# K and Q projections of a cross-attention kernel: the last 64 features with the weights' high and low parts in one stationary

## The reference, cut to what matters

```python
q = _split_heads(hidden_states @ w_q, HEADS)            # (16*256, 320) @ (320, 320)
k = _split_heads(text @ w_k, HEADS)                     # (.., 512) @ (512, 320)
v = _split_heads(text @ w_v, HEADS)
out_text = _merge_heads(_sdpa(q, k, v))
out_ip = _merge_heads(_sdpa(q, k_ip, v_ip, mask=mask_ip))
out = (out_text + out_ip) @ w_out + b_out + residual
```

## Time and profile before

| | |
|---|---|
| three timed runs | 524.48, 525.25, 527.94 us, median 525.25 |
| the profiled execution | 523.65 us, span 521.8 us (1.85 us lie around the span) |
| mean granted TensorE clock | 0.984 |
| TensorE matmul busy | 476.5 us, 91% |
| VectorE busy | 380.1 us, 73% |
| ScalarE busy | 275.9 us, 53% |
| GpSimd busy | 134.6 us, 26% |
| stages, from the span's start | lone tiles to 57 us, batch -1 to 79, batches 0 to 11 to 429, the rest to 521.8 |

### The profile page before, as it was taken

The page is one execution under the profiler, slowest core; times in us unless marked ns, Lnnn a source line. Parts: engine busy times, 40 slices in busy tenths (PEclk is TensorE's granted clock), DMA queues, the critical chain, the costliest instruction groups (busy, mean ns, idle before and its releaser), DMA issues.

```text
span 521.8 us, 11039 instructions
## 1 busy us (share of the span) xinstructions
PE 476.5 (91%) x4306; PEld 321.1 (62%) x4306; DVE 380.1 (73%) x687; ACT 275.9 (53%) x355; POOL 134.6 (26%) x208
## 2 busy tenths in 40 slices
PE   2998668999999999999999999999999998798895
PEld 2786535676667756676667756676667755454542
DVE  4833466877877797877877797877877779899732
ACT  3643025555655565455655555455655456466670
POOL 6250000313221140313222140314212220432431
PEclk9999797999999999999999999999999999999998
DMA  8999985858593967758593958757594937273011
GB/s 270 333 227 314 360 289 180 286 174 265 166 335 102 328 194 202 263 167 276 179 333 93 334 186 221 245 169 268 179 302 129 319 125 244 87 262 109 9 53 50
DMA packets 94036, 112.61 MB, mean 216 GB/s; under 512 B 14320, under 2 KB 72736, under 8 KB 93984
## 3 DMA queue, kind: packets, MB, share of 16 engines
q1 hardware_dynamic: 92960, 109.57, 65.9%
q0 software_dynamic: 1024, 2.34, 1.9%
HBM read 73.28 MB, written 38.63 MB: 214 GB/s over the span
## 4 chain that ended last, share of the span: by engine, by line
issue 56%; POOL 21%; PE 10%; DMA 5%; SPq 3%; DVE 2%; ACT 1%; POOLq 0%; ACTq 0%
POOL o_turned L411 10%; POOL o_all L416 7%; POOL x_all L405 4%; PE score_q L650 1%; DMA v_rows<-v_out 1%; PE pv L762 1%; PE score_q L651 1%; PE score_q L652 1%; DMA max_rows<-row_buf 1%; SPq L226 1%; PE pj L771 1%; DMA probs<-in_wk 1%; PE score_t L748 1%; DMA raw<-in_ctxT 1%; DMA q_parts<-qk_out 1%
## 5 line engine op out<-in xcount | busy, mean ns | idle before, releaser
L562 DVE TENSOR_REDUCE max_cols<-score_q 128x4 fp32r<-128x992 f32 x155 | 183.1, 1181 | 86.1 <-PE score_q L693 85.1
L494 ACT ACTIVATE probs<-score_t 128x1024 f32<-128x1024 f32 x160 | 163.3, 1021 | 145.8 <-PE score_t L748 145.8
L762 PE MATMUL pv<-probs,v_cur 128*32 128x256 f32 x1920 | 120.2, 383 | 0.6 <-ACT probs L494 0.6
L411 POOL TENSOR_TENSOR o_turned<-o_turned,inv_cols 128x256 f32<-128x256 f32 x80 | 53.9, 674 | 155.3 <-DVE inv_cols L606 155.3
L771 PE MATMUL pj<-wo_sb,o_all 128*128 128x320 f32 x192 | 70.5, 477 | 9.6 <-DVE out_sb L618 5.8
L762 PEld LDWEIGHTS pv<-probs,v_cur 128*32 128x32 f32 x1920 | 54.3, 109 | 39.1 <-issue 1.0
L405 POOL TENSOR_TENSOR x_all<-x_all,bias_sb 128x640 f32<-128x640 f32 x16 | 24.9, 1559 | 202.0 <-DMA x_all<-in_x 202.0
L748 PE MATMUL score_t<-q_stack,k_stack 64*128 64x256 f32 x440 | 55.8, 332 | 11.2 <-ACT probs L494 7.9
L748 PEld LDWEIGHTS score_t<-q_stack,k_stack 64*128 64x128 f32 x440 | 33.1, 186 | 52.2 <-issue 36.1
L603 DVE STREAM_TRANSPOSE o_turned<-o_all 128x512 f32<-128x512 f32 x80 | 55.8, 698 | 11.9 <-ACT o_all L486 11.9
L486 ACT ACTIVATE o_all<-pv 128x512 f32<-128x512 f32 x80 | 47.8, 598 | 27.3 <-PE pv L762 27.3
(11 more groups left out here) (152 smaller groups left out, 635.2 us busy)
## 6 DMA issues: line engine op xcount, KB each, us to landing
k_stack<-k_parts SPq DMA_DIRECT2D x33, 320.0 KB, 5.2
q_stack<-q_parts SPq DMA_DIRECT2D x33, 320.0 KB, 6.6
v_rows<-v_out SPq DMA_DIRECT2D x32, 320.0 KB, 6.7
v_cur<-v_rows SPq DMA_DIRECT2D x16, 640.0 KB
q_parts<-qk_out SPq DMA_DIRECT2D x32, 256.0 KB, 4.0
k_parts<-qk_out SPq DMA_DIRECT2D x32, 248.0 KB, 5.9
raw<-in_ctxT SPq DMA_DIRECT2D x14, 512.0 KB, 5.3
x_all<-in_x SPq DMA_DIRECT2D x16, 320.0 KB, 7.5
```

The lines of the kernel that those rows point to most:

```text
L411: pool.tensor_tensor(out, out, inv_cols[:, n % SLOTS, :].unsqueeze(2).broadcast_to([P, 2 * S // 32, DH]), ALU.mult).then_inc(scaled, 1)
L494: nc.scalar.activation(probs[:, slot(t % 2, p), :], score_t[:, :], ACT.Exp, scale=SCALE)\
L562: nc.vector.tensor_reduce(out=max_cols[:, h, :, at:at + 4:2].rearrange("p t e -> p e t"), in_=both[:, :, :, 0:TEXT], op=ALU.max, axis=AX.X ...
L762: last = mm(pv[32 * t:32 * t + 32, at:at + S], values_of(u, kind, 4 * k + t), probs[:, slot(u, 2 * k + t // 2), a:a + S], start=kind != 1, ...
```

## The change

The weights' parts are laid out anew. `wq_hi` and `wq_lo` become one array `wq_hl`, and `wk_hl` changes its layout: for each chunk, 256 columns high, 256 columns low (`wide`), then 64 columns high and 64 low of the tail, side by side (`narrow`). The full blocks (j = 0, 1, 7, 8) still do the three matmuls of each chunk. For a tail, one matmul with 128 stationary columns multiplies high and low weights by the high moving operand at once: rows 0 to 63 of the bank get the high part's product, rows 64 to 127 the low part's. One more matmul with 64 columns adds high weights by low operand to rows 0 to 63. A K tail is then 8 matmuls and not 12, a Q tail 5 and not 8.

The two row halves have to be added. ScalarE still copies rows 0 to 63 as the high part. VectorE now takes two instructions: rows 64 to 127 minus the high part into `tail_rest` (L565 of the new kernel), a wait on its own semaphore `tail_step`, and rows 0 to 63 plus `tail_rest` into the low part (L568). The weights' high and low parts of K and Q are made by two instructions each and not one, for the wide and the narrow columns.

```diff
+        def wide(w, s):
+            return w[:, :, 2 * P * s:2 * P * s + 2 * P]
+        def narrow(w, s):
+            return w[:, :, 4 * P + TAIL * s:4 * P + TAIL * s + TAIL]
...
-            high(wk_hl[:, 0], wk_raw, ld["wk"], 16)
+            def high_parts(w, raw, loaded, value):
+                act.wait_ge(loaded, value)
+                nc.scalar.activation(wide(w, 0), raw[:, :, 0:2 * P], ACT.Copy)
+                nc.scalar.activation(narrow(w, 0), raw[:, :, 2 * P:D], ACT.Copy).then_inc(w_high, 1)
+            high_parts(wk_hl, wk_raw, ld["wk"], 16)
...
-                nc.vector.tensor_tensor(qk_out[0:r, j % 3, 1, :], tile_bank(n)[0:r, :],
-                                        qk_out[0:r, j % 3, 0, :].bitcast(f32), ALU.subtract)\
-                    .then_inc(lo_done, 1)
+                high_part, low_part = qk_out[0:r, j % 3, 0, :].bitcast(f32), qk_out[0:r, j % 3, 1, :]
+                if j % 3 == 2:
+                    nc.vector.tensor_tensor(tail_rest[:, :], tile_bank(n)[TAIL:P, :], high_part, ALU.subtract)\
+                        .then_inc(tail_step, 1)
+                    dve.wait_ge(tail_step, 2 * g + j // 3 + 1)
+                    nc.vector.tensor_tensor(low_part, tile_bank(n)[0:r, :], tail_rest[:, :], ALU.add)\
+                        .then_inc(lo_done, 1)
+                else:
+                    nc.vector.tensor_tensor(low_part, tile_bank(n)[0:r, :], high_part, ALU.subtract)\
+                        .then_inc(lo_done, 1)
...
-            low(wk_hl[:, 1], wk_raw, wk_hl[:, 0])
+            def low_parts(w, raw):
+                n_low[0] += 1
+                dve.wait_ge(w_high, n_low[0])
+                nc.vector.tensor_tensor(wide(w, 1), raw[:, :, 0:2 * P], wide(w, 0).bitcast(f32), ALU.subtract)
+                nc.vector.tensor_tensor(narrow(w, 1), raw[:, :, 2 * P:D], narrow(w, 0).bitcast(f32), ALU.subtract)\
+                    .then_inc(w_low, 1)
+            low_parts(wk_hl, wk_raw)
...
+            def narrow_tile(out, w, c, x_hi_, x_lo_, start, stop):
+                both = lambda: mm(out, w[:, c, 4 * P:4 * P + 2 * TAIL], x_hi_, start=start, stop=stop)
+                high_low = lambda: mm(out[0:TAIL, :], narrow(w, 0)[:, c, :], x_lo_, start=False, stop=False)
+                if x_lo_ is None:
+                    return both()
+                if start:
+                    both()
+                    return high_low()
+                high_low()
+                return both()
```

More of the change, by code:

```diff
@@ L23 @@
 MT_ROWS = [128, 128, 64]
+TAIL = MT_ROWS[2]
 VW = 2 * D
@@ L66, in xattn @@
         x_lo = sb("x_lo", [P, 2, GT], f32r)
-        wq_hi = sb("wq_hi", [P, XC, D], f32r)
-        wq_lo = sb("wq_lo", [P, XC, D], f32r)
-        wk_hl = sb("wk_hl", [P, 2, CC, D], f32r)
+        wq_hl = sb("wq_hl", [P, XC, 2 * D], f32r)
+        wk_hl = sb("wk_hl", [P, CC, 2 * D], f32r)
         wv_hl = sb("wv_hl", [P, 2, CC, D], f32r)
         qk_out = sb("qk_out", [P, 3, 2, GT], f32r)
+        tail_rest = sb("tail_rest", [MT_ROWS[2], GT])
         v_out = sb("v_out", [P, 2, VW])
@@ L139, in xattn @@
         hi_done, lo_done = sem("hi_done"), sem("lo_done")
+        tail_step = sem("tail_step")
         v_evac = sem("v_evac")
@@ L457, in _ @@
             high(wv_hl[:, 0], wv_raw, ld["wv"], 16)
-            high(wq_hi[:, :, :], wq_raw, ld["wq"], 48)
+            high_parts(wq_hl, wq_raw, ld["wq"], 48)
             tile(1)
@@ L579, in _ @@
             low(wv_hl[:, 1], wv_raw, wv_hl[:, 0])
-            low(wq_lo[:, :, :], wq_raw, wq_hi[:, :, :])
+            low_parts(wq_hl, wq_raw)
             tile(1)
@@ L652, in three, with wide_tile @@
                 return mm(out, w_hi, x_lo_, start=False, stop=stop)
+            def wide_tile(out, w, m, c, x_hi_, x_lo_, start, stop):
+                cols = slice(m * P, m * P + P)
+                mm(out, wide(w, 0)[:, c, cols], x_hi_, start=start, stop=False)
+                last = mm(out, wide(w, 1)[:, c, cols], x_hi_, start=False, stop=stop and x_lo_ is None)
+                return last if x_lo_ is None else mm(out, wide(w, 0)[:, c, cols], x_lo_, start=False, stop=stop)
+            def narrow_tile(out, w, c, x_hi_, x_lo_, start, stop):
[8 more added lines that the diff above has]
+                return both()
             def k_tile(g, m, out):
-                r, cols = MT_ROWS[m], slice(m * P, m * P + MT_ROWS[m])
                 for c in range(CC):
@@ L657, in k_tile @@
                         pe.wait_ge(c_split, 2 * g + c // 2 + 1)
-                    last = three(out[0:r, :], wk_hl[:, 0, c, cols], wk_hl[:, 1, c, cols], c_hi[:, c, :],
-                                 c_lo[:, c, :], c == 0, c == CC - 1)
+                    x_, ends = (c_hi[:, c, :], c_lo[:, c, :]), (c == 0, c == CC - 1)
+                    last = wide_tile(out, wk_hl, m, c, *x_, *ends) if m < 2 else narrow_tile(out, wk_hl, c, *x_, *ends)
                 last.then_inc(tile_ready, 1)
@@ L667, in q_tile @@
             def q_tile(g, m, out):
-                r, cols = MT_ROWS[m], slice(m * P, m * P + MT_ROWS[m])
-                for c in range(2):
-                    three(out[0:r, :], wq_hi[:, c, cols], wq_lo[:, c, cols], x_hi[:, c, :], x_lo[:, c, :],
-                          c == 0, False)
-                mm(out[0:r, :], wq_hi[:, 2, cols], x_hi[:, 2, :], start=False, stop=False)
-                mm(out[0:r, :], wq_lo[:, 2, cols], x_hi[:, 2, :], start=False, stop=True)\
-                    .then_inc(tile_ready, 1)
+                for c in range(XC):
+                    x_, ends = (x_hi[:, c, :], x_lo[:, c, :] if c < 2 else None), (c == 0, c == XC - 1)
+                    last = wide_tile(out, wq_hl, m, c, *x_, *ends) if m < 2 else narrow_tile(out, wq_hl, c, *x_, *ends)
+                last.then_inc(tile_ready, 1)
             def query_scores(b, p):
```

## The result

The changed kernel takes 529.58 us (median of 16 runs, 526.04 to 534.90), the kernel before, run beside it, 525.59 us (16 runs): a ratio of 1.0066 [1.0043, 1.0089], 4.0 us slower. Forecast were +2.4 us, "the same, on the slow side", in a range of 521 to 533. It came out so, with a loss somewhat larger. Measured once more in a later group of runs, the ratio was 1.013 [1.0099, 1.0161], 6.4 us between the medians; the two intervals don't overlap, so the size of the loss is known to some 2 us only.

A forecast was written before the change was run, and what follows sets the result against it. TensorE is busy 91%, but VectorE's `finish` was taken to set the pace once a batch, ahead of L771. Terms +2.15 - 0.15 + 0.4 = +2.4 us on 525.25 gave 527.6 us; range 521 to 533.

The forecast's parts named there:

- K tail, +0.43 in each of five batches: Even batches 2 to 10: VectorE's extra instruction makes `finish` and the output projection L771 0.43 us later, 2.15 us in all.
- The extra instruction, 0.68 + 0.03: VectorE's second 64x512 instruction per tail: 0.68 us plus 0.03 wait, 0.71 us a tail, 11.4 us in all.
- Q tails, -0.15: p = 9 of odd batches: TensorE's 0.69 us mostly becomes waiting; 0.1 us at most won in batches 1 and 5.
- last rival: VectorE pays at every hosted tail, at p = 0 to 2 of even batches: +8.5 us, 533.7 us; chance 0.12.
- The drain: Alternating 128 and 64 stationary columns drains TensorE: start steps 0.39, not 0.23 us; +4.2 us, 529.4 us; chance 0.12.
- I take 0.4: Lone tiles at the start: VectorE's added work delays the special keys; bounds 0 and 0.66 us, 0.4 us taken.
- I count nothing for the clock: TensorE's granted clock, 1.00 in batches 0 to 11 despite idle times up to a microsecond: no cost counted.

The follow-up runs named there:

- e1: Changed kernel with one VectorE instruction per tail, the high product of rows 0 to 63 left out of the low part; 526.37 us, ratio 1.0029.
- e2: Kernel before with one more 64x512 VectorE subtraction, waited for, ahead of each tail's low part, all matmuls kept; 531.25 us, ratio 1.0092.
- e3: Changed kernel with `finish` ahead of the hosted tile's low part on VectorE at p = 6; 524.74 us, ratio 0.9949.
- e8: e3 with ScalarE's split of the context's second half at p = 9 and not p = 8; 522.86 us, ratio 0.9932.
- e10: Changed kernel with only batch 0's K tail (tile 22) done as before; 532.01 us, ratio 1.0112.
- e5: Changed kernel with only hosted tails joined, the three lone tails as before; 532.88 us, ratio 1.0147; again 536.53 us, 1.0203.
- e6: Changed kernel with only the lone tails joined, all hosted tails as before; 529.12 us, ratio 1.0071.
- e4: Kernel before with `finish` ahead of the hosted tile's low part on VectorE at p = 6; 523.03 us, ratio 0.9942.
- e7: e4 with ScalarE's split of the context's second half at p = 9 and not p = 8; 520.65 us, ratio 0.9874.
- e9: e8 with only the K tails of batches 2 to 10 joined, all other tails as before; 521.41 us, ratio 0.9905.

## Why the prediction was right, and what it had wrong

- **K tail, +0.43 in each of five batches.** Right in mechanism and nearly in size: from the exp of p = 5 on, the pairs of batches 6, 8 and 10 stand 0.91 us earlier at p = 6, 0.46 earlier at p = 7 and 0.45 later from p = 8 on; the stretch grew by 2.6 us where 2.15 were forecast, since batch 2 lost some 0.3 more and batch 4 0.1. e1, e2 and e3 show the cause.
- **The extra instruction, 0.68 + 0.03.** 0.69 and 0.68 us with 0.03 between them. Reading rows 64 to 127 into rows 0 to 63 costs nothing extra.
- **Q tails, -0.15.** -0.1 in sum, and that is in part luck: single odd batches differ by -0.7 (batch 11, which splits no context) to +0.8 us (batch 9), and over the profiles in which nothing was moved Q goes from 31.3 to 34.8 us. Why nothing arrives was right: with the context's DMA out of the way (e8) the 0.7 us arrive, and are then paid at p = 0 to 5, at the place of the last rival.
- **The drain.** Refuted: steps of 0.23 us.
- **"I take 0.4" for the lone tiles, with bounds of 0 and 0.66.** Too small, as far as the profiles can tell. In the two main profiles the special keys start 1.00 us later (24.26 to 25.26) and the first exp of batch 0 1.9. Both scatter. Over six profiles with the lone tiles as before the special keys start at 24.1 to 25.3, mean 24.7, over the six with the changed ones at 24.6 to 25.7, mean 25.3: 0.6 us, close to the 0.66 worked out. The first exp comes at 78.8 to 81.4, mean 80.1, with the lone tiles as before, and at 80.1 to 82.5, mean 81.0, in the seven with them joined (e1 among them). So about +1 us is what the profiles bear out. In the main pair SyncE's queue did swallow part of the delay, as the prediction held possible: the V tiles were stored 2.5 us late, the issue of `q_parts` at 40.76 came at 41.05, 0.3 late. But later issues were late again, and on the whole nothing was saved by it.
- **"I count nothing for the clock".** The reason given was that TensorE had idle times of up to a microsecond in batches 0 to 11 and kept its clock; the change made idle times of 1.4 us at the start, and of 2.1 us in batch 0 where the collision came. A loss of clock is there. Beside the kernel before on the same chip, every kernel with more joined tails than the K tails of batches 2 to 10 has a mean clock lower by 0.002 to 0.008 (changed 0.972 and e10 0.974 against 0.977, e1 and e3 0.972 against 0.980, e5 0.975, e6 0.973 and e8 0.970 against 0.978); the others, e2, e4, e7 and e9, lie between 0.002 under it and 0.001 over it. What it costs isn't shown. 0.005 of 530 us is an estimate of 2.7 us of TensorE's work, and a bound, since part falls where TensorE waits. The fall near 27 us in particular costs nothing that shows at batch 0: the four profiles with it reach the first exp at 80.1 to 81.1 us, e3 and e8 without it at 81.8 and 82.5 (these two have 10.2 us and not 6.8 at 1.2 GHz from 53 us on). And e1 has the low mean clock without that fall and with 0.67 us of idle time in its place.
- **What remains open.** 4.0 us in the medians are 2.6 from K and about 1 from the start; the rest is of the size of batch 0's collision in some of the runs, and that this is it wasn't shown. In the later group of runs the loss is 6.4 us, and the 2.4 us more have no account beyond the collision in its one profile. Nor is it explained why e5 is slower than the changed kernel in both measurements: its two profiles lose most in batches 12 to 14 (64.2 and 65.6 us against 62.6 and 62.1), the second with 6.8 us at 1.2 GHz there. The collision itself was found by sorting profiles, and no kernel that moves GpSimd's instruction was run.

The verdict and the main term were right: K is 2.6 of the 4.0 us. Of the 1.6 us between the forecast and the medians, 0.45 are K's second and third batch and some 0.6 the start. That the rest was small in the first measurement is luck as much as foresight, since the second one lies 2.4 us higher.

## What to carry to other kernels

Before matmuls are traded for an instruction on another engine, follow both to the next place where the engines meet: here TensorE's 0.9 us ended at a bank that VectorE freed 0.43 us later. Moving `finish` ahead of the tail's low part adds no instruction and made the kernel before 0.6% faster (0.9942), where the change made it slower. An engine that arrives earlier at an unchanged wait stands idle for longer; look at the granted clock behind such a wait, in more than one profile.
